# Layer 0's first batch: GpSimd's fills behind the weight split, and group 0's stacks issued part by part

## What is computed

```
x = x + attention0(layernorm(x))          # 16 heads of 16, causal, this study's place
x = x + mixture_of_experts(layernorm(x))  # 8 experts, top 2 by each output
x = x + attention1(layernorm(x))          # 16 query heads of 128, 4 key heads
x = x + gated_mlp(layernorm(x))           # 2048 wide, 4-bit weights

qkv = einsum('bsd,od->bso', layernorm(x), w_project)
att = softmax(causal(q @ k.T / sqrt(16)));  out = (att @ v) @ w_out.T
```

## Time and profile before

| | |
|---|---|
| median of 3 runs | 1190.35 us (1189.95 to 1190.75) |
| profiled execution, its own time | 1194.26 us |
| span of the profiled execution | 1192.5 us |
| mean granted TensorE clock over the span | 0.927 |
| busy over the span: PE, DVE, ACT, POOL | 1005.9, 857.1, 498.4, 311.4 us |

### The profile page before, as it was taken

How to read it: one execution, slowest core, us unless ns; L and a number is a source line. 1 busy time by engine, 2 the same in 40 slices (tenths; PEclk the granted TensorE clock), 3 DMA queues, 4 the chain that set the end, 5 groups by cost and what they waited for, 6 DMA issues and landing times. The chain is left out here.

```text
span 1192.5 us, 19875 instructions
## 1 busy us (share of the span) xinstructions
PE 1005.9 (84%) x6885; PEld 588.9 (49%) x6960; DVE 857.1 (72%) x1556; ACT 498.4 (42%) x972; POOL 311.4 (26%) x337
## 2 busy tenths in 40 slices
PE   3698989888788798797487898898989799999997
PEld 1344545445444454353134474474657465556554
DVE  5677767643999899999967754746582776777766
ACT  2154444354464564646334313314230344444443
POOL 3243424531532524333320202203135400000000
PEclk9799989998899798898789898898897999999999
DMA  6622222101001000010000000001001000000000
GB/s 172 112 73 90 64 81 67 58 2 45 1 1 44 1 27 18 0 45 1 0 18 6 23 11 16 21 2 26 11 24 46 22 1 18 1 18 0 18 1 18
DMA packets 37088, 35.87 MB, mean 30 GB/s; under 512 B 8585, under 2 KB 33417, under 8 KB 37009
## 3 DMA queue, kind: packets, MB, share of 16 engines
q1 hardware_dynamic: 35728, 33.79, 9.8%
q10 hardware_dynamic: 1280, 1.05, 0.7%
HBM read 27.28 MB, written 6.29 MB: 28 GB/s over the span
## 5 line engine op out<-in xcount | busy, mean ns | idle before, releaser
L883 DVE TENSOR_REDUCE bm<-ps 128x4 f32<-128x512 f32 x160 | 102.1, 684 | 33.4 <-PE ps L603 31.7
L782 ACT ACTIVATE pt<-ps 128x1024 f32<-128x1024 f32 (+1 forms) x96 | 82.1, 882 | 72.5 <-PE ps L679 71.9
L1753 DVE TENSOR_TENSOR qk_lo<-ps,qk_hi 128x512 bf16<-128x512 f32 x80 | 54.9, 687 | 67.1 <-ACT qk_hi L1646 60.8
L2001 ACT ACTIVATE g<-ps 128x512 f32<-128x512 f32 x64 | 38.2, 597 | 134.1 <-PE ps L1948 107.4
L156 POOL TENSOR_TENSOR mag_w<-stage 128x512 f32<-128x512 fp8e4 x24 | 26.4, 1100 | 224.7 <-DVE stage L143 224.7
L2051 DVE SCALAR_TENSOR_TENSOR g<-g,ps 128x512 f32<-128x512 f32 x64 | 44.0, 688 | 54.5 <-ACT g L2001 54.2
L599 PE MATMUL ps<-ks,qs 96*128 96x512 bf16 (+3 forms) x256 | 66.7, 314 | 12.4 <-DMA ks<-scratch_k 7.7
L1646 ACT ACTIVATE qk_hi<-ps 128x512 bf16<-128x512 f32 x80 | 47.8, 599 | 69.4 <-PE ps L1515 69.4
L547 POOL TENSOR_SCALAR_AFFINE_SELECT pt<-pt 128x256 f32<-128x256 f32 (+1 forms) x96 | 47.2, 498 | 110.9 <-ACT pt L782 110.3
L1515 PE MATMUL ps<-wp_hi,oT_hi 128*128 128x256 bf16 x256 | 71.1, 278 | 5.0 <-DVE oT_lo L1746 5.0
L1964 PE MATMUL ps<-ew_hi,it_hi 128*128 128x256 bf16 x256 | 69.8, 273 | 6.1 <-DVE it_lo L2067 6.1
(11 more groups left out here) (272 smaller groups left out, 2840.9 us busy)
## 6 DMA issues: line engine op xcount, KB each, us to landing
qs<-scratch_q SPq DMA_DIRECT2D x64, 64.0 KB, 2.6
ks<-scratch_k SPq DMA_DIRECT2D x48, 64.0 KB, 2.6
q_next<-in_w_qkv SPq DMA_DIRECT2D x4, 768.0 KB, 4.4
X<-in_x SPq DMA_DIRECT2D x4, 512.0 KB, 7.0
w_next<-in_router_w SPq DMA_DIRECT2D x4, 512.0 KB, 3.7
w_next<-in_expert_w SPq DMA_DIRECT2D x4, 512.0 KB, 4.6
p_next<-in_w_proj SPq DMA_DIRECT2D x4, 512.0 KB, 5.4
out<-X SPq DMA_DIRECT2D x8, 256.0 KB, 2.3
```

Of the source, the lines that this page charges most:

```text
L782: act.activation(pt[kt][:, heads[0]:heads[-1] + 1, :], src, ACT.Exp).then_inc(s_exp, 1)
L883: ins = dve.tensor_reduce(bm[:, 2 * g + i // 5, 4 * (i % 5):4 * (i % 5) + 4], src.rearrange("p (k q) -> p k q", k=4), AX_X, ALU.max)
L1753: dve.tensor_tensor(qk_lo[:, k, h, :], bank(QK_BANK[m]), qk_hi[:, k, h, :], ALU.subtract).then_inc(s_qklo, 1)
```

## The change

```diff
@@ -331,6 +331,7 @@
         wsplit_hi, wsplit_lo = st.sem("wsplit0_hi"), st.sem("wsplit0_lo")
         s_stat, s_mv, s_rstd = st.sem("stat0"), st.sem("mv0s"), st.sem("rstd0s")
         s_xn, s_xhi, s_xlo, s_qkhi = st.sem("xn0s"), st.sem("xhi0"), st.sem("xlo0"), st.sem("qkhi")
+        s_first = [st.sem(f"first_part{k}") for k in range(4)]
         s_scr, s_stk = [st.sem(f"scr{n}") for n in (0, 1)], [st.sem(f"stack{g}") for g in range(NG)]
         s_zero, s_ones = st.sem("zero_tile"), st.sem("constant_rows")
 
@@ -376,15 +377,18 @@
                 batch(b, False, False)
             batch(B - 1, False, True)
 
+        def stack_part(eng, g, n, part):
+
+            heads = slice(HG * g, HG * (g + 1))
+            scr, dst, hi_lo_rows = ((scratch_q, qs, ((0, 2), (1, 3))), (scratch_k, ks, ((0, 1), (2, 3))))[n]
+            for r in hi_lo_rows[part]:
+                eng.dma_start(dst[HD0 * r:HD0 * (r + 1), heads, :],
+                              scr[part].rearrange("(h d) t -> d h t", d=HD0)[:, heads, :]).then_inc(s_stk[g], 16)
+
         def stack_rows(eng, g, which):
-
-            heads = slice(HG * g, HG * (g + 1))
             for n in which:
-                scr, dst, hi_lo_rows = ((scratch_q, qs, ((0, 2), (1, 3))), (scratch_k, ks, ((0, 1), (2, 3))))[n]
-                for part, rows in enumerate(hi_lo_rows):
-                    for r in rows:
-                        eng.dma_start(dst[HD0 * r:HD0 * (r + 1), heads, :],
-                                      scr[part].rearrange("(h d) t -> d h t", d=HD0)[:, heads, :]).then_inc(s_stk[g], 16)
+                for part in range(2):
+                    stack_part(eng, g, n, part)
 
         with nc.Block() as block:
 
@@ -436,11 +440,24 @@
                 for r in (SHIFT, SHIFT + 1):
                     sp.dma_start(ks[r:r + 1, :, :].rearrange("o h (j q) -> o (h j) q", q=P), ones_row[:, :]
                                  ).then_inc(s_ones, 16)
-                for half_ in range(2):
-                    copy_parts(0, [START.index(("qk", m)) for m in range(4)], half_)
-                    wait_alone(sp, s_scr[half_], 64, passed_sp)
-                    for g in (2 * half_, 2 * half_ + 1):
-                        stack_rows(sp, g, (0,))
+                for k in range(4):
+                    n, part = divmod(k, 2)
+                    if part:
+                        sp.wait_ge(s_taken, START.index(("qk", 2 * n)) + 1)
+                    else:
+                        sp.wait_ge(s_qkhi, n + 1)
+                    sp.dma_start((scratch_q, scratch_k)[n][part, 0:P, :], (qk_hi, qk_lo)[part][:, 2 * n, :]
+                                 ).then_inc(s_first[k], 16)
+                for k in range(4):
+                    wait_alone(sp, s_first[k], 16, passed_sp)
+                    n, part = divmod(k, 2)
+                    stack_part(sp, 0, n, part)
+                sp.sem_inc(s_scr[0], 64)
+                stack_rows(sp, 1, (0,))
+                copy_parts(0, [START.index(("qk", m)) for m in range(4)], 1)
+                wait_alone(sp, s_scr[1], 64, passed_sp)
+                for g in (2, 3):
+                    stack_rows(sp, g, (0,))
                 shift_group(0, 0, START.index(("turn", 0)))
 
                 def batch(b, first, last):
@@ -524,7 +541,7 @@
                     pool.tensor_tensor(rstd[:, :], rstd[:, :], half[:, :], ALU.pow).then_inc(s_rstd, 1)
 
                 root(0)
-                pool.wait_ge(s_rstd, 2)
+                wait_alone(pool, wsplit_lo, 1, passed_pool)
                 pool.memset(ones4[:, :], 0.0).then_inc(s_ties, 1)
                 pool.wait_ge(s_ties, 1)
                 pool.memset(ones4[0:4, :], 1.0).then_inc(s_ties, 1)
@@ -556,10 +573,13 @@
             def _(pe):
                 pe.wait_ge(const, 4)
 
-                def three(out, lhs, rhs):
+                def three(out, lhs, rhs, arrived=None):
 
                     n = 0
                     for c in range(KC):
+                        if arrived is not None:
+                            pe.wait_ge(s_xhi, arrived + c + 1)
+                            pe.wait_ge(s_xlo, arrived + c + 1)
                         for a, b_ in ((0, 0), (0, 1), (1, 0)):
                             mm = pe.matmul(out, lhs[a](c), rhs[b_](c), start=(n == 0), stop=(n == 3 * KC - 1))
                             n += 1
@@ -573,10 +593,8 @@
 
                 def queries_keys(b, m, out):
 
-                    pe.wait_ge(s_xhi, 2 * b + 2)
-                    pe.wait_ge(s_xlo, 2 * b + 2)
                     return three(out(), [lambda c: w_hi[:, c, P * m:P * (m + 1)], lambda c: w_lo[:, c, P * m:P * (m + 1)]],
-                                 [lambda c: xT_hi[:, c, :], lambda c: xT_lo[:, c, :]])
+                                 [lambda c: xT_hi[:, c, :], lambda c: xT_lo[:, c, :]], arrived=2 * b)
 
                 def value_rows(half_, out):
                     for t in (2 * half_, 2 * half_ + 1):
@@ -766,7 +784,7 @@
                     take(0, n, n % NB0, kind, arg)
                 for half_ in range(2):
                     act.wait_ge(s_scr[half_], 64)
-                    for g in (2 * half_, 2 * half_ + 1):
+                    for g in (2 * half_, 2 * half_ + 1)[1 - half_:]:
                         stack_rows(act, g, (1,))
 
                 def exponentials(b, g, u):
```

## The result

The changed kernel takes 1178.80 us (median of 6 executions, 1178.10 to 1183.73), the kernel before 1191.61 (6 executions, 1189.95 to 1195.89): a ratio of 0.9893, with a 95% interval of 0.9868 to 0.9919, so 12.8 us less, between 9.7 and 15.7. The forecast was 1182.4, 7.95 us less than the 1190.35 of three executions. On which side of the edge a single median falls is chance; that the gain is several us above 7.95 is not.

The account below looks back on a forecast made before the run. The first stretch was taken as bound by a chain of dependences ahead of TensorE's work. Terms 3.6 + 0.85 + 2.0 + 1.5 = 7.95 us, off 1190.35, gave 1182.4 us; range 1179.0 to 1186.5.

Parts of the forecast that it names:

- Steps 1 and 2: Batch 0's start: fills moved behind the weight split, products started on x's first transposed half; 4.45 us together.
- Rival (b): The fill did not hold xn, or now holds a low half: 1185 to 1186; chance 0.22 shared with Rival (a).
- step 1: GpSimd's fills moved behind the weight split, so batch 0's four xn take 1.35 us instead of 4.94: 3.6 us.
- Steps 4 and 5: Batch 0's scratch copies and stacks: group 0 part by part on SP, first maxima 2.5 us sooner, second stacks 2.0.
- Rival (a): DMA queue drain or SP issue is the limit, not the parts' arrival: about 1185.5; chance 0.22 shared with Rival (b).
- Step 6: Batch 0's shift row, issued after SP's second stacks, keeps its landing length; scores start at 43.0 instead of 49.47.
- Step 3: Later three batches: three products moved into each wait for x transposed, 0.5 us each, 1.5 us in all.
- Rival (c): Moved starts lengthen TensorE's stretches at the lower clock, making the kernel slower: 1193 or more; chance 0.03.
- Rival (d): More than forecast: the products' pace rises at once and the drain relieves more, 1178 to 1179; chance 0.04.

Follow-up runs that it names:

- after_again: The unaltered changed kernel measured a second time, on another chip: 1180.68 us, ratio 0.9902 to the kernel before.
- halves_batch0: Changed kernel, but products start on the first half of x transposed in batch 0 only; later batches wait for both: 6.9 and 8.2 us less than the kernel before.

## Why the prediction was off

- *Steps 1 and 2*, batch 0. Transposes forecast at 11.2 and found at 11.24; first product 13.9 and 13.89; low halves and qk_lo unstretched. Right. The Trainium skill's rule (SBUF — State Buffer, Who interferes with whom) held in both its parts: 3.82 us for an xn beside the fill before, 0.69 us for a tensor_tensor with an input in PSUM beside the same fill now. Rival (b) is out. Alone, step 1 gave 3.84 us at the first maxima but 4.68 at the scores, and 4.8 by the times (3.2 to 6.3). The small fills took 2.40 us beside the weight split and 2.08 in the changed kernel, so "without either being stretched" was a misreading as far as they go, without effect on the path.
- *Steps 4 and 5*, the stacks. First stack 20.4 forecast, 20.59 found; first maxima 26.4 and 26.79; second stacks 31.5 and 31.58; alone, 2.0 us forecast and 2.03 found at the scores. Right where it entered the sum; the 2.5 us for the first maxima were 1.91 alone and 2.1 (6.53 less 4.45) in the whole change. Rival (a) is out. The Trainium skill (DMA: Bandwidth & Descriptors, Issuing engines are not separate DMA queues) says that DMAs started from several engines save the sequencer's time alone. From that the prediction worked out a loss of 1.8 us for SP's longer list, which would have put the first maxima near 28.2; the 26.79 don't bear such a loss out. The two versions with two queues don't settle what ScalarE's queue could save with group 0 alone, since group 1's stacks ran beside.
- *Step 6*, the scores at 43.0: found at 42.69, a gain of 6.78 where 6.45 was forecast. At this point the forecast had lost 0.3 us.
- *Step 3 is the term that was mis-sized.* "At most 0.65 us, 2.0 in all … I count 0.5 each, 1.5 us." Alone it is 2.5 us by the times (1.2 to 3.8), and 2.4 by the traces when the clock's share is taken off; in the trace of the changed kernel the work brought forward is 0.64, 0.65 and 1.06 us. Two things were wrong in it. I discounted 0.65 to 0.5 us, though nothing in the profile asked for it: the full length of the three products was brought forward each time. And I priced them at full clock, 0.22 us each, in all batches; where TensorE stands at the lower level they take 0.43 us, so 2.0 was not the most that the step could give. On top of the rest it looks larger, 3.5 to 5.9 us (6.9 and 8.2 against 12.8 and 11.7), and why is open.
- *Rival (c)*, that moved starts lengthen the stretches at the lower clock, did not come: the mean granted clock over the span is 0.9285 in the six executions of the changed kernel and 0.9272 in after_again's five, against 0.9271 to 0.9278 for the kernel before on four chips. (By its own half a us, 15.9 us more at the lower level would have cancelled 7.95, not 17.)
- *Rival (d)*, 1178 to 1179, named the time of the first measurement and not its cause. The products' pace rose at about 18.2 instead of 22.3 us, so it moved with the work and not ahead of it, and the drain gave at the scores what was forecast.
- *The base*. The forecast subtracted from 1190.35, a median of three. The kernel before has since given medians of 1191.61 to 1192.74 in 6 to 17 executions. Against such a base the same 7.95 us would have given about 1184, and the miss of the gain, 3.7 and 4.8 us, would have shown in full; a low base hid a part of it.

What stays open: about 2 of the 12 us. The terms as measured in the traces are 6.8 us up to the scores, 0.3 by the first v copy and 2.4 to 3.4 in the later batches, 9.5 to 10.5 in all; the times say 12.8 and 11.7, with intervals that begin at 9.7 and 8.6. Of the miss of 4.8 or 3.7 us, step 3 is 0.9 to 1.9, steps up to the scores 0.3, the first v copy 0.3; the rest is not explained. That products thrown away in the same gaps take about 2 us off the time, and nothing off the batches in the traces, shows that the time of this kernel can move by such an amount without work brought forward. Whether the half waits have the same effect beside the work that they bring forward, no run here separates.

## What to carry to other kernels

Where a stretch is a chain of dependences ahead of one that TensorE fills, each link can be priced from its own row, and at the scores the sum of the whole change held to 0.3 us (the fills alone were 1.1 us off there). Work that is moved into a gap is worth its own length at the clock of that place, so price it at both levels. In this kernel products with no use, put into TensorE's gaps, took about 2 us off the time by a way that the traces don't show; it is worth a trial, with enough executions to tell 2 us, and no rule. Small urgent DMAs should be issued ahead of the bulk that is not yet wanted (scores 3.1 us earlier here). And spreading stacks over two queues can make the first group later, when the second queue is ready late and stacks that are wanted later run beside.

## What had not been expected of the hardware

- Three products whose result is thrown away, in gaps of 1.3 to 1.9 us, made the kernel before 2.6 us faster (interval 1.2 to 4.1) with nothing else changed; six waits in the same place of halves_batch0 did nothing (6.9 us of gain, beside 6.9 and 8.2 without). The traces show no gain in the batches where the products stand.
- Fourteen stacks of 64 KB issued from two queues in 3.4 us landed 2.3 to 5.1 us after issue (median 4.1), and eight from one queue in 3.2 us landed 2.5 to 2.9 us after it.
